# Router products by column group, statistics first, w2 turned in the prologue, and row moves, zeros and loads in other places

## What is computed

```python
xn = _layernorm(x)                                   # over the 128 features
# attention, H=16 heads of DQ=64, NB=10 position bases, window 128
Q, K, V = xn@Wq+bq, xn@Wk, xn@Wv ;  R = xn@Wr+br     # R: 10 numbers for each head and row
extra   = einsum('bhtn,ntp->bhtp', R, D_ntT)         # bias that depends on the distance t-p
W       = softmax(Q@K.T/8 + causal mask + extra)
attn    = (W@V) @ Wproj + bproj
# experts, 8 of them, the best 2 of each row, 128 -> 512 -> 128
logits  = xn @ router_w.T ;  top 2, softmax of the two
experts = sum over the two of weight * (gelu(xn@w1[e].T+b1[e]) @ w2[e].T + b2[e])
```

## Time and profile before

| | |
|---|---|
| median of 3 runs | 1437.1 us (1433.1 to 1441.4) |
| the profiled execution | 1442.45 us, span of its instructions 1440.7 |
| TensorE busy | 1349.7 us (94%), granted clock 0.972 on average |
| VectorE, ScalarE, GpSimd busy | 885.6 (61%), 935.8 (65%), 876.8 (61%) |
| DMA | 274.96 MB, 191 GB/s |

### The profile page before, as it was taken

How to read it: one execution, slowest core, us unless ns; L and a number is a source line. 1 busy time by engine, 2 the same in 40 slices (tenths; PEclk the granted TensorE clock), 3 DMA queues, 4 the chain that set the end, 5 groups by cost and what they waited for, 6 DMA issues and landing times. The chain is left out here.

```text
span 1440.7 us, 35076 instructions
## 1 busy us (share of the span) xinstructions
PE 1349.7 (94%) x10669; PEld 1144.0 (79%) x10669; DVE 885.6 (61%) x3633; ACT 935.8 (65%) x2963; POOL 876.8 (61%) x1652
## 2 busy tenths in 40 slices
PE   4789997999999999999699999999999999999997
PEld 3578786887877877788599999998888888877885
DVE  3329886776677777677421122115788788877876
ACT  1247775776777777677555445445777777777774
POOL 5555653866777776777232222234777777777773
PEclk9669999999999999999899999999999999999999
DMA  6326767777777787786745555554787877777773
GB/s 195 106 78 196 206 184 217 229 211 208 211 225 205 216 236 226 205 234 193 204 140 167 169 163 163 170 144 121 205 223 209 218 211 211 204 212 204 219 208 87
DMA packets 457090, 274.96 MB, mean 191 GB/s; under 512 B 21660, under 2 KB 437319, under 8 KB 456904
## 3 DMA queue, kind: packets, MB, share of 16 engines
q1 hardware_dynamic: 448712, 255.93, 63.6%
q0 software_dynamic: 8192, 16.79, 3.8%
HBM read 124.19 MB, written 133.19 MB: 179 GB/s over the span
## 5 line engine op out<-in xcount | busy, mean ns | idle before, releaser
L890 ACT ACTIVATE prob<-logit,low 128x128 f32<-128x128 f32 x1024 | 401.2, 395 | 64.4 <-DVE low L1193 56.6
L768 POOL TENSOR_SCALAR prob<-prob,inv 128x128 f32<-128x128 f32 x512 | 187.4, 366 | 208.0 <-DVE inv L1210 203.4
L1193 DVE CUSTOM_DVE_ANT_0 logit<-ps,extra 128x128 f32<-128x128 f32 x1024 | 255.5, 287 | 94.2 <-PE ps L1449 38.0
L1449 PEld LDWEIGHTS ps<-qk 64*128 64x128 f32 x2048 | 168.7, 190 | 60.1 <-issue 47.8
L1175 DVE TENSOR_TENSOR probT<-ps,keep 128x512 f32<-128x512 f32 x256 | 175.7, 686 | 58.3 <-PE ps L1436 33.9
L1449 PE MATMUL ps<-qk 64*128 64x256 f32 (+1 forms) x2048 | 205.6, 341 | 0.0
L1468 PE MATMUL ps<-probT,val 128*64 128x256 f32 (+1 forms) x2048 | 194.7, 332 | 8.5 <-DVE acc L1251 7.9
L890 ACT ACTIVATION_READ_ACCUMULATOR prob<-logit,low 128x1 f32 x1024 | 194.0, 189 | 0.0
L880 ACT COPY qk<-ps 128x512 f32<-128x512 f32 x256 | 150.2, 587 | 56.5 <-PE ps L1347 27.8
L770 POOL TENSOR_SCALAR prob<-prob,inv 128x128 f32<-128x128 f32 x512 | 186.4, 364 | 0.0
L1468 PEld LDWEIGHTS ps<-probT,val 128*64 128x64 f32 x2048 | 128.2, 136 | 60.4 <-ACT val L844 4.8
(11 more groups left out here) (178 smaller groups left out, 2638.6 us busy)
## 6 DMA issues: line engine op xcount, KB each, us to landing
skew<-gst SPq DMA_DIRECT2D x384, 256.0 KB
extra<-skew SPq DMA_DIRECT2D x256, 256.0 KB
w2b<-w_d SPq DMA_DIRECT2D x39, 320.0 KB, 3.4
rT<-r_hi SPq DMA_DIRECT2D x128, 80.0 KB
w1raw<-w_d SPq DMA_DIRECT2D x39, 258.0 KB, 2.8
placed<-x_place SPq DMA_DIRECT2D x39, 256.0 KB, 3.2
y_place<-yrow SPq DMA_DIRECT2D x39, 256.0 KB, 2.2
rT<-r_lo SPq DMA_DIRECT2D x64, 80.0 KB
```

What stands on the lines that cost most here:

```text
L768: nc.gpsimd.tensor_scalar(prob[:, h, 0:P], prob[:, h, 0:P], inv[:, h, 0:1], 1.0, ALU.mult, ALU.mult).then_inc(norm_made, 1)
L890: ins = nc.scalar.activation(prob[:, h % PB, cols], logit[:, h % LB, cols], ACT.Exp, scale=-1.0, bias=low[:, h % LB, t:t + 1], accum_out=t ...
L1193: ins = nc.vector.tensor_tensor_reduce(out=logit[:, h % LB, cols], in0=ps[:, b + n, cols], in1=extra[:, h, cols], scale=1.0, scalar=BIG, o ...
L1449: mm = nc.tensor.matmul(ps[:, S_BANK[pair % 2][n], cols], qk[rows, pair % 2, 0, q], qk[rows, pair % 2, 1, k], start=True, stop=True)
```

## The change

- Router: `rwT` is zero-padded to 32 columns and is now the stationary operand; four products of 512 columns write partitions 0, 32, 64 and 96 of one bank (`router(j)`, four instead of sixteen), ScalarE copies the result, `router_back(j)` turns it by four transposes, and VectorE keeps the eight useful columns of each.
- All statistics are taken, and the second variances made, before any centring of Wq. TensorE does turn(0), Wq's sums, turn(1), unit r, Wk's sums, turns 2 and 3, Wv's sums. X's quarter 3 is loaded ahead of Wk. Three buffers for normalised blocks; VectorE makes eight of them instead of four.
- w2 (2 MB) is loaded in one transfer in the prologue, turned on TensorE beside blocks 5 to 8, and stored in one transfer. Its buffer shares memory with `extra`, so SP waits for the last turn before the first read; the turned copy shares memory with the routing's buffers, so VectorE waits for the store before the first sequence.
- w1 is turned by two w units in each of sequences 0 to 3 (d = 1 and 2). Sequences 4 to 16 have none.
- Zero blocks two at a time at q = 0 to 3; pads two at a time at q = 14 to 17; row moves from q = 19; rows of X are loaded four tiles at a time, two steps ahead, into two buffers.
- GpSimd: add_bias behind the norms; at d = 0 all row moves stand behind round_weights.
- VectorE takes the counts one place earlier in its list.

```diff
-    XR = 4
+    XR = 2
...
         COUNT_AT = 2
-        TURN_AT = [i for i in range(2 * NX + 1) if i != COUNT_AT]
+        TURN_AT = {4 * i + d: 2 * i + (d == 2) for i in range(NX // 2) for d in (1, 2)}
...
-        SPREAD_FROM, SPREAD_DS = 18, 4 * (HALF - 1) + 1 - 18
+        SPREAD_FROM, SPREAD_DS = 19, 4 * (HALF - 1) + 1 - 19
...
             load_x(2)
+            load_x(3)
             sp.dma_start(wqk_r[:, 1, :], Wk).then_inc(wk_in, 16)
-            load_x(3)
...
+            sp.dma_start(w2_raw[:, :, :], w2.rearrange("e h f -> h e f")).then_inc(w2_in, 16)
...
-            def zero_pads():
+            def zero_pads(first_expert):
                 sp.wait_ge(owner_made, 1)
-                for e in range(NX):
+                for e in (first_expert, first_expert + 1):
...
             def others(q):
+                if q - 1 in TURN_AT:
+                    store_turn(TURN_AT[q - 1])
+                    if TURN_AT[q - 1] + 2 < NX:
+                        load_turn(TURN_AT[q - 1] + 2)
+                for n in range(SURE, PLACES):
+                    if (n - SURE) // 2 == q:
+                        zero_block(n)
+                if 14 <= q < 14 + NX // 2:
+                    zero_pads(2 * (q - 14))
                 for n in range(BLOCKS):
+                    if rows_at[2 * n] - 2 == q:
+                        fetch_rows(n)
...
             spread_weights(0)
+            sp.dma_start(wproj[:, :, :], Wproj.rearrange("(k d) e -> d k e", d=P)).then_inc(proj_in, 16)
+            sp.wait_ge(filled, 16)
+            write_unit(0, *POSITIONS_AHEAD[0])
+            sp.wait_ge(w2_psum, NX)
+            read_unit(0, *POSITIONS_AHEAD[0])
+            positions(0, POSITIONS_AHEAD[1:])
+            sp.wait_ge(w2_made, NX)
+            sp.dma_start(w2_d[:, :, 0:FF].rearrange("e p c -> p e c"), w2t[:, :, :]).then_inc(w2_put, 16)
+            sp.dma_start(bproj_bc[:, :], bproj.partition_broadcast(P)).then_inc(bproj_in, 16)
             load_turn(0)
             load_turn(1)
...
-        XN_DVE = (6, 9, 12, 15)
+        XN_DVE = (5, 6, 8, 9, 11, 12, 14, 15)
...
                     if heads:
-                        if 4 * i + d < BLOCKS:
-                            add_bias(4 * i + d)
-                        moves(4 * i + d, 0)
+                        if d > 0:
+                            moves(4 * i + d, 0)
                     if here(i, d - 1, heads, start):
                         pool.wait_ge(inv_made, i * QUADS + d)
                         norms(i, d - 1, 0)
                         norms(i, d - 1, 1)
-                    if heads:
-                        moves(4 * i + d, 1)
+                    if heads and 4 * i + d < BLOCKS:
+                        add_bias(4 * i + d)
                     if d == 0 and heads and more:
                         round_weights(i + 1)
+                    if heads:
+                        if d == 0:
+                            moves(4 * i, 0)
+                        moves(4 * i + d, 1)
...
             deviations(0, 0, 16)
-            for k in range(4):
-                turned(k)
+            turned(0)
+            turned(1)
             unit(0)
+            turned(2)
+            deviations(1, 16, TILES)
             high_weights(0, 1.0)
-            deviations(1, 16, TILES)
+            turned(3)
             high_weights(1, -SCALE)
...
             take_stats(1)
             take_stats(2)
+            take_stats(3)
+            dve.wait_ge(stats_made, 4)
+            variances(16, TILES)
...
+            keep_logits(3)
+            dve.wait_ge(lg_made, 4)
+            dve.wait_ge(w2_put, 16)
...
+            def router(j):
+                pe.wait_ge(xnT_made, 4 * j + 4)
+                wait_from(pe, lgT_made, j)
+                for c in range(PER):
+                    k = PER * j + c
+                    mm = nc.tensor.matmul(ps[32 * c:32 * c + 32, LGT_BANK, :], rwT[:, :], xnT[:, k * BANK:(k + 1) * BANK],
+                                          start=True, stop=True, skip_group_check=True)
+                mm.then_inc(lgT_psum, 1)
+
+            def router_back(j):
+                pe.wait_ge(lgT_made, j + 1)
+                wait_from(pe, lg_made, j)
+                for t in range(PER):
+                    mm = nc.tensor.transpose(ps[:, LG_BANK, t * P:(t + 1) * P], lgT[:, t * P:(t + 1) * P], ident[:, :])
                 mm.then_inc(lg_psum, 1)
+
+            def turn_w2(e):
+                wait_from(pe, w2_made, e - 2)
+                for c in range(FC):
+                    mm = nc.tensor.transpose(ps[:, W2_BANK[e % 3], c * P:(c + 1) * P], w2_raw[:, e, c * P:(c + 1) * P], ident[:, :])
+                mm.then_inc(w2_psum, 1)
...
             for k in range(4, BLOCKS):
                 turn(k)
-                if k > 4:
-                    router(k - 1)
+                if k % 4 == 1:
+                    router(k // 4 - 1)
                 if k - 3 < len(START):
                     unit_taken(pe, k - 4)
                     unit(k - 3)
...
+                if 5 <= k < 9:
+                    turn_w2(2 * (k - 5))
+                    turn_w2(2 * (k - 5) + 1)
+                if k % 4 == 2:
+                    router_back(k // 4 - 1)
```

More of the change, by code:

```diff
@@ L527, in others, with fetch_rows @@
-            def others(q):
[L530 to L543, removed]
+            def fetch_rows(n):
+                wait_from(sp, spread[n % XR], n // XR * 128)
+                sp.dma_start(xrow[:, n % XR, :, :], x_v[:, PER * n:PER * n + PER, :]).then_inc(xrow_in[n % XR], 16)
@@ L1033, in _, with norm_block, low_weights, keep_logits @@
             take_stats(2)
+            take_stats(3)
+            dve.wait_ge(stats_made, 4)
+            variances(16, TILES)
+            def norm_block(k):
+                dve.wait_ge(xnT_psum, k - 2)
+                for n in range(PER):
+                    ins = nc.vector.tensor_scalar(xn[:, k % 3, n, :], acc[:, PER * k + n, :],
+                                                  mean[:, PER * k + n:PER * k + n + 1],
+                                                  rstd[:, PER * k + n:PER * k + n + 1], ALU.subtract, ALU.mult)
+                ins.then_inc(xn_dve, 1)
+            def low_weights(w, scale):
+                dve.wait_ge(qk_high, w + 1)
+                nc.vector.scalar_tensor_tensor(out=wqk_lo[:, w, :], in0=wqk_r[:, w, :], scalar=scale,
+                                               in1=wqk_hi[:, w, :].bitcast(F32), op0=ALU.mult,
+                                               op1=ALU.subtract).then_inc(qk_low, 1)
+            def keep_logits(j):
+                dve.wait_ge(lg_psum, j + 1)
+                src = ps[:, LG_BANK, :].rearrange("p (t c x) -> p t c x", t=PER, c=PER)
+                nc.vector.tensor_copy(lg[:, 16 * j:16 * j + 16, :].rearrange("p (c t) e -> p t c e", c=PER),
+                                      src[:, :, :, 0:NX]).then_inc(lg_made, 1)
             dve.wait_ge(mean_psum, 3)
@@ L1512, in _ @@
             turn(0)
-            turn(1)
-            router(0)
-            turn(2)
-            router(1)
-            turn(3)
-            router(2)
-            router(3)
-            pe.wait_ge(wr_split, 2)
-            unit(0)
             pe.wait_ge(wq_in, 32)
@@ L1526, in _ @@
                 column_sums(Q_MEAN_BANK[k], wqk_r[:, 0, k * BANK:(k + 1) * BANK], bq_row[:, k * BANK:(k + 1) * BANK])
+            turn(1)
+            pe.wait_ge(wr_split, 2)
+            unit(0)
             pe.wait_ge(wk_in, 16)
@@ L1529, in _ @@
                 column_sums(K_MEAN_BANK[k], wqk_r[:, 1, k * BANK:(k + 1) * BANK], None)
+            turn(2)
+            turn(3)
             pe.wait_ge(wv_in, 16)
@@ L1545, in _ @@
             keys(0, 0)
+            router_back(3)
             keys(0, 1)
-            pe.wait_ge(wv_centred, 2)
-            pe.wait_ge(lg_made, 1)
+            pe.wait_ge(w2_made, NX)
+            pe.wait_ge(lg_made, 4)
             for i in range(B):
```

185 lines of the change are left out of this document (104 added, 81 removed).

## The result

The changed kernel takes 1448.5 us and the kernel before 1433.8 (medians of 17 runs each): ratio 1.0088, 95% interval 1.0069 to 1.0107. It is slower, by 14.7 us between the medians and by 12.6 by the ratio. Forecast was 1456, 18.9 above the kernel before.

The account below looks back on a forecast made before the run. TensorE was taken to bound the attention sequences; prologue and early-sequence gains, GpSimd-order waits, later savings and new clock drops summed to +18.9 us, carried over to the median of 1437.1: 1456 us, range 1425 to 1478.

Parts of the forecast that it names:

- GpSimd's order: At d = 0, three or four row moves before the norms stall TensorE: +30.7 us in sequences 5 to 17, +24.8 in 18 to 30.
- no idle time: Sequences 18 to 30: TensorE was taken as full, so none of the +24.8 us of new waits is given back.
- rival 3: Row moves in a row cost GpSimd little: -43, 1394 us; second way, TensorE not truly full behind the wait: 1425; chance 0.16.
- Clock drops: After the twelve new stalls of about 3 us, 60% lose 1.7 us to a lower clock: +12.3 us, between 0 and 20.
- The gains in sequences 5 to 17: rT waits -11.3 us, w units -5.3, w_turned waits -2.6, other waits covered -3.6, old clock drops -5.1.
- The prologue: Phase two starts at 40 us instead of 53.4 and the keys near 73.5 instead of 88.29: -14.8 us.
- At half clock: Prologue's second half: TensorE stays at half clock, so phase two takes 32 us.
- rival 2: Prologue: 512-column routers and sums raise the clock, phase two shrinks by some 12 us, 1444 in all; chance 0.08.
- Rival 5: The prologue ends on the w2 store or the first reads: up to +10 us, 1466; chance 0.05.
- Sequences 0 to 4: Pads in pairs -9.5 us, w1 units +1.8, zero blocks, pads and row loads +1.5; by stage -6.2.
- Two at a time, 2.5 us, fit into what SP had spare: Sequences 0 to 4: pads in pairs fit SP's spare 2.8 us, removing the stall and its half clock: -9.5 us.
- Two signs named in the forecast: If right, rT waits are nearly gone and no stall stands near the pads.

Follow-up runs that it names:

- e1: Changed kernel with GpSimd's steps of a sequence in the order of the kernel before; 1403.5 us, ratio 0.9762 to the kernel before.
- e4: Changed kernel with the routers of before (16 products of 8 columns a block, no turning back) in the new places; 1466.4 us.
- e3: Changed kernel with the load of bproj_bc issued ahead of w2 instead of behind the store of the turned w2; 1444.5 us.
- e2: Kernel before with only GpSimd's new order, and its own table of row moves; 1451.9 us, ratio 1.0122.
- e8: e1 with bproj_bc loaded before SP's first read into extra and VectorE's wait for the w2 store moved behind the first logits; 1401.2 us.
- e10: e8 with the eight pad transfers issued by GpSimd instead of SP, two at each of q = 14 to 17; 1393.8 us.
- e7: e1 with all eight pad transfers at q = 14 instead of two at each of q = 14 to 17; 1401.1 us.
- e11: e10 with the seven zero blocks also issued by GpSimd, one at each place from q = 2; 1389.6 us.
- e6: e1 with w1 turned in one unit a sequence (sequences 0, 1 and 3 to 8) instead of two; 1405.1 us.
- e9: e8 with zero blocks one at each place from q = 2 instead of two from q = 0, still on SP; 1400.5 us.

## Why the prediction was right, and where it was wrong

**GpSimd's order: right.** In sequences 5 to 30 55.5 us of stalls were forecast and 51.7 measured (52.7 with two small ones earlier), at the very places: twelve with four moves behind r_lo, twelve with three, one of 0.3. Each was 0.1 to 0.2 us shorter than forecast. The order with its clock drops costs 29.6 us in the first stretch and 19.1 in the second (e1). The forecast had 36.9 there, less the 14.9 that it was to cover, and 31.0. The second stretch wasn't as full as "no idle time" said: TensorE waited 6.4 us there before and 8.3 in e1, and in the changed kernel for the stalls alone (21.5 up to r_raw(30)), so that they cover the other waits. This is a part of rival 3's second way. Its first, cheap moves, is refuted: a move occupies GpSimd for about 1.0 us and the next starts 1.3 after it.

**Clock drops: the size right, by some luck.** Of twelve stalls of about 2.8 us six were followed by half clock (near 270, 304, 539, 1051, 1150 and 1253), five of 3.4 us and one of 6.8, so about 11.9 us lost for 12.3 forecast. After the same twelve stalls e4 had six drops too, but e3 only three, of 3.4 us each (5.1 lost).

**The gains in sequences 5 to 17: size right, reason half wrong.** -27.9 was forecast for rT, w units, w_turned, the old drops and 3.6 of other waits. e1 against before gives 377.8 - 405.3 = -27.5. But 14.9 of it (rT and the 3.6) was to come because the new wait covers these waits, and e1 has no such wait: its waits for rT in this stretch are 2.5 us all the same, where before has 13.2. e2 shows that the order alone covers them too (3.1). So either part of the change takes them away, and it could be counted only once. In e1 SP issues rT 1.5 and 2.9 us behind r_lo in sequences 5 and 6, where before had 4.3 and 6.2; which of the edits to SP's list does it was not tried.

**The prologue: mechanism right, size wrong.** The start of phase two was off by 0.8 us. "At half clock", which I took over from the earlier trace rows, was the failed step: rival 2 happened, the phase took 22.8 us and not 32, and r_raw(0) gained 25.5, not 14.8. e4 shows that the clock hangs on the routers' form. Rival 5 happened beside it: 4.25 us for xq_lo and half clock from 71.7 to 81.9. The forecast's own terms also don't give its 73.5: 40 and 32.1 are 72.1, and the 1.4 that is left over is as much as the waits that the 32.1 already has. And the thirteen routers of phase two before are twelve, which no term uses.

**Sequences 0 to 4: sign wrong.** "Two at a time, 2.5 us, fit into what SP had spare" failed. Taking the pads off SP gained 8.8 us in this stage (e8 to e10), where pairs were to cost nothing, and pairs are at most a few us better than all at once (e7), so most of the -9.5 was never there. Two signs named in the forecast failed with it: the waits for rT are 13.9 us and not nearly gone, and a stall of 5.3 stands behind the pads. I had taken the spare from a kernel that came into this stage 25 us later: in it SP issued rT 0.0 us behind the end of r_lo in sequence 0, in the changed one 4.2, and e4, with its late prologue, again 0.0. That the shorter prologue ate the spare fits this, e8 and e4's 10 us, each by one execution. The zero blocks cost about 4 more (e10 to e11, 172.5 to 168.7, one execution each), where +1.5 stood for them and more; w1 nothing (e6). The order's share in this stage can't be read from one execution each: kernels with SP's list of the change took 174 to 183.5 us for it.

**The sum** came out 11 us too high by profiles, 4 by medians and 6 by the ratio, and that it came so near is partly luck: -11 in the prologue and -11 and -7 in the long stretches met +20 in sequences 0 to 4 (and -2.6 around the experts), each against its forecast.

## What to carry to other kernels

Count, for every engine that executes in order, what a reordering puts between the arrival of an input and the work that the bounding engine waits for, in pieces of measured length; here that count gave the stalls to 0.1 to 0.2 us. An item that a queue issues can cost by standing ahead of something urgent, not by its bytes: here spreading it in the same queue moved the loss (e9), giving it to an engine with idle time removed it (e10). And when one stage is shortened, the slack that later stages had before it must be worked out anew.

## What the runs showed of the chip

Four fp32 products of 512 columns in four column groups of 32 took 1.07 us in all at the granted clock 1.00, where a single one takes 1.8 at 0.50, so 0.9 at 1.00 by estimate: they ran side by side. An indirect transfer of 128 rows held GpSimd for 0.95 to 1.08 us in most cases, 1.24 at most; a plain one of 256 KB to a row offset from a register held it for 0.72 to 0.85 (e10), and SP for 0.97 (in pairs) to 1.26 (eight in a row, before). The granted clock was 0.54 on average from 70 to 95 us in e4, though TensorE was busy for 91% of it, and 1.00 from 40.9 to 62 in the changed kernel at 78%: here busy time alone doesn't tell the clock.
